# A decoder layer on one core: another interleaving in the order table, fifteen warm-up transposes instead of twenty-five, and one drain less

## The reference

```python
x = layernorm(x + attn(x))        # causal: softmax(q k / sqrt(16)) v, with biases, then Wo, bo
x = layernorm(x + xattn(x, ctx))  # 64 context tokens, key mask from batch 0's lengths
x = layernorm(x + ffn(x))         # down(silu(gate(x)) * up(x)), inner width 1024
# ffn: activations rounded to 8 bits by row, weights rounded to -1, 0, 1 with one scale each
```

## Time and profile before

| | us |
|---|---|
| median of 3 executions (864.41 to 867.02) | 865.58 |
| the profiled execution | 864.41 |
| its span, first to last instruction | 862.7 |
| PE busy | 807.5 |
| DVE busy | 674.9 |
| ACT busy | 578.9 |
| POOL busy | 387.2 |

### The profile page before, as it was taken

The page is one execution under the profiler, slowest core; times in us unless marked ns, Lnnn a source line. Parts: engine busy times, 40 slices in busy tenths (PEclk is TensorE's granted clock), DMA queues, the critical chain, the costliest instruction groups (busy, mean ns, idle before and its releaser), DMA issues.

```text
span 862.7 us, 21746 instructions
## 1 busy us (share of the span) xinstructions
PE 807.5 (94%) x8207; PEld 389.9 (45%) x8235; DVE 674.9 (78%) x1179; ACT 578.9 (67%) x759; POOL 387.2 (45%) x621
## 2 busy tenths in 40 slices
PE   7888999999999999999999999999999999999875
PEld 5433334343554434534464344643645443445533
DVE  5899798658967799778998589874898948836698
ACT  2277865467874688555885679756697569964486
POOL 4724465446343257532634544372634603343345
PEclk8899999999999999999999999999999999999999
DMA  7713124301223212201221111130130100010001
GB/s 227 202 40 99 38 62 105 94 2 27 55 53 98 62 37 49 78 1 26 72 66 39 35 53 45 39 86 20 39 85 17 50 2 1 2 50 1 2 2 49
DMA packets 47814, 45.50 MB, mean 53 GB/s; under 512 B 9698, under 2 KB 43874, under 8 KB 47714
## 3 DMA queue, kind: packets, MB, share of 16 engines
q1 hardware_dynamic: 43698, 39.12, 16.4%
q0 software_dynamic: 1536, 3.15, 1.6%
q10 hardware_dynamic: 2480, 1.84, 0.8%
HBM read 14.55 MB, written 4.19 MB: 22 GB/s over the span
## 4 chain that ended last, share of the span: by engine, by line
PE 75%; DVE 12%; ACT 7%; issue 3%; DMA 1%; POOL 1%; SPq 1%; POOLq 0%; DVEq 0%
PE ps L988 14%; PE ps L1003 14%; PE ps L800 10%; PE ps L962 7%; PE ps L815 5%; DVE shift L1317 5%; PE ps L934 4%; PE ps L861 3%; PE ps L946 3%; ACT probs L1106 3%; PE ps L789 2%; PE ps L891 2%; DVE shift_h L1317 2%; PE ps L903 2%; PE ps L886 2%
## 5 line engine op out<-in xcount | busy, mean ns | idle before, releaser
L1106 ACT ACTIVATE probs<-ps 128x1024 f32<-128x1024 f32 (+3 forms) x384 | 296.2, 810 | 123.6 <-PE ps L988 121.3
L1317 DVE TENSOR_REDUCE shift<-ps 128x2 f32<-128x1024 f32 (+2 forms) x224 | 248.6, 1144 | 51.3 <-PE ps L962 28.8
L988 PE MATMUL ps<-q_stack,k_stack 64*128 64x512 bf16 (+3 forms) x1536 | 174.4, 325 | 10.4 <-ACT probs L1106 3.3
L1003 PE MATMUL ps<-probs,v_aug 128*32 128x512 f32 (+3 forms) x1536 | 155.7, 495 | 0.1
L689 POOL TENSOR_SCALAR_AFFINE_SELECT probs<-probs 128x512 f32<-128x512 f32 x128 | 80.6, 638 | 156.7 <-ACT probs L1106 155.9
L962 PE MATMUL ps<-k_stack,q_stack 64*128 64x512 bf16 (+3 forms) x768 | 115.3, 327 | 9.8 <-ACT probs L1106 3.5
L988 PEld LDWEIGHTS ps<-q_stack,k_stack 64*128 64x128 bf16 x1536 | 54.8, 94 | 121.9 <-ACT probs L1106 45.4
L1317 DVE TENSOR_REDUCE shift_h<-ps 128x4 bf16<-128x512 f32 (+2 forms) x96 | 96.9, 1044 | 15.7 <-PE ps L969 15.2
L962 PEld LDWEIGHTS ps<-k_stack,q_stack 64*128 64x128 bf16 x768 | 39.6, 94 | 97.7 <-ACT probs L1106 36.3
L1003 PEld LDWEIGHTS ps<-probs,v_aug 128*32 128x32 f32 x1536 | 34.8, 108 | 42.9 <-issue 31.4
L966 PE MATMUL ps<-causal,pick_h 64*128 64x128 bf16 x512 | 53.5, 217 | 0.0
(11 more groups left out here) (186 smaller groups left out, 1376.9 us busy)
## 6 DMA issues: line engine op xcount, KB each, us to landing
q_stack<-part_sb SPq DMA_DIRECT2D x168, 64.0 KB, 2.0
k_stack<-part_sb SPq DMA_DIRECT2D x144, 64.0 KB, 2.1
xT<-in_x_cols SPq DMA_DIRECT2D x8, 512.0 KB, 4.0
xt<-in_x SPq DMA_DIRECT2D x8, 512.0 KB, 3.9
out_x<-xt SPq DMA_DIRECT2D x7, 512.0 KB, 2.9
k_stack<-part_sb POOLq DMA_DIRECT2D x48, 64.0 KB, 2.1
q_stack<-shiftT SPq DMA_DIRECT2D x128, 1.0 KB
q_stack<-part_sb ACTq DMA_DIRECT2D x24, 64.0 KB, 2.5
```

The source lines that it names most:

```text
L988: mm = pe.matmul(ps[:, u.banks[i], 0:BANK - off], k_stack[rows, part, h, kb * P:(kb + 1) * P], q_stack[rows, part, c, h, off:BANK], start= ...
L1003: mm = pe.matmul(ps[DV * i:DV * (i + 1), SUM_BANK, off:BANK], v_aug[:, kb, at:at + DV], probs_of(b, n)[:, i, :], start=first, stop=last)
L1106: act.activation(probs_of(b, n)[:, 2 * p:2 * p + 2, :], pair(u)[:, :, 0:BANK - off], ACT.Exp).then_inc(probs_ready, 1)
L1317: dve.tensor_reduce(to[:, :, pairs[0]:pairs[-1] + 1, qb % TH], pair(u)[:, :, 0:len(pairs) * w].rearrange("p j (h w) -> p j h w", w=w), AX. ...
```

## The change

Three edits. The string `ORDER` is replaced by another interleaving of the same 1917 units; 793 of the 1212 units that write banks get other banks. `stir` runs 15 transposes instead of 25. The `pool.drain()` behind `make_masks` is gone. Of the string only the first line stands here:

```diff
 ORDER = (
-    "ffwr6sfffr0sgr6sr1r0r6sr2m01m45m23r6ggm45m01m23m45r6ffffm01m23gr4m01m56m23a01a45am01a23w6a45m01fffaa23a45am2"
+    "r6sr5sr6sr5r6sgr5m01gm23m45r6m01ggm45m01r6fm23m01m23wfm01m45r3fm01a45w6r3m01a45fffam23m01a45w6a23afm45fa01oa"
...
                         make_masks()
-                        pool.drain()
...
                     if b == 0 and u.idx == 0:
-                        stir(u, 25)
+                        stir(u, 15)
```

More of the change, by code:

```diff
@@ L47 @@
[L47 to L66, removed]
@@ new lines @@
+    "am45r6m01ooa23m45a01o23m45sa01om23a45m01a23a45m01oa23m01a45ga23m01a45m23oam01wa45oa23aa01oa45rm23am01a45a23a"
+    "m45a23m01a45gam23om01m45m23r6m01oom23oa45m01ra23o45am01a23a45oaa23m45a01m23goom01awa45oa23aa01m45r6rm01m23a4"
+    "5aa01om45m23a01o01oaa23m45a01em23eaa01m45oa23m01ooogm45a23o01m45a23p01om23m45bm01p6p5a01a23a45opm01m23r6m01p"
+    "a45a23om45rp01m23m45p6m01m23p5pp6p1p0a23bgaop6gm45a01pr3p6p5a01p2p6aa34a01op6m01p24arm01r6m01ra23p45p02p45r6"
+    "p45a01p23m01aa45op23p01a45om23p01om45a23m01p6m23oa01m45p6o01a23a45oa01goa23pm45rm01r6a23m45a01ppaoa23pa45pap"
@@ new lines @@
+    "rom01m23r6a01a45oaa01m23a45p01m45aom23p6m01m45p3p2om01oop6m45gp3o01p2p6p5p3p2a01gpa34m56apr2xppgp1p0a34a56op"
+    "m12aa34a56pppar0p45a23p6p1oa45apa23a01m45ppr6pam01p23p5p6a23a01m45ooop6aa23a01po45aoa23oopa01ppm23p45p6m01p2"
+    "3p6p3papp01otoa45a23m01p6xo45m01ea23p6a23pa01a45oa23om01a45a23pa01m45oam23p45m01a23m45p6m01m23p5pp6p1p0a23op"
+    "6aa23pm45ba01am23a01p6p1p0a23oap6a23m45a01op6oom01p24om01r6m01p23p04rp23r6a23p01p45m01a23p45rp01o23om45p01om"
+    "23a01m45p6m01m23a45p6a01a23gopa45pa01am23m45a23m01m45a23apoa01a23aa45poa01pm23paa45m01r6m23oom01p45m23a01m45"
@@ new lines @@
+    "p6m23op1gm45ap0m23orp6m45p1p0m23p6o45p1p0a23p6m45a01paoa23a45ppapp6p1a23a45ar0pa23pm45oom01prpa23om45aor6o01"
+    "p23p5p6a01m23a45m01aa23a45goapa23m01a45pppop23m45p6p1ap0a45oopoa23pppp01p6ro45m23oa45m01p23p6m45p3ppa01a45p6"
+    "p3p2p01oca45m01p6m23p5pa01a23gm45oa01pm23r6m01a45aa23ora45am01p23om45a01m23p6a01m23p5pp6tp3aa01p2a45ap6a01m4"
+    "5opea23m01oooa45p6p3a01p2a45p6o01a23p6gm45p02m45r6m45p01p24rbp01op01m23p45m01a23p45a01p23om45p01m23om45a01p6"
+    "m01a23am45p6a01m23a45poapa01a23m45r6am01a23m45a23gom01paa23oa45pm23opaopm01m45rr6a23ga01m45p23m01om45m23p6p1"
@@ new lines @@
+    "r0xp5p6p1m23m45p6ap0o23p1p6p5m23a01ooa45aa23a01appppp6m45a23ga01ap6oopa45pppop23p6p1pr0a45par6ppo23p45p1p6a2"
+    "3m45a01ap6a23m01pa45oaa45a23pm01om45oppp23m01p6om45m23xp01p6a45p1ppp23oa45a01m23p6p5o01pa23oa45a01om23pa45oa"
+    "01am23a45om01a23p45am01om23m01p6m23m01p5pp6p3p2a01a45oaa01p6m45pa23m01aoa23a45tp6p1p0a23p6m45r1ep6m23bop04rm"
+    "23r6p01rp24p01r6op01p23a45o01op23a01gp45a23m01p45orm23a45m01p6m23a45m01p6a23m01a45poaa23pm01a45aoa23a45oam23"
+    "a01a45m01aga45pa23pr6m01apm23m45oa01opom23oa45m01ap23m45a01a23rp6m01m23m45p1p0ap6p3o12m45p0p6gp2p3p5a01oa23a"
@@ new lines @@
+    "a45ppppp6p1m23poa45oaa01oa23poppp45p6p1am23r6a01a45pppapgp23p6o01p5oa01p6a45aa23pa01pom45ppom23p01op6om45a23"
+    "p01p6m45ro23oa01m45p6ppa01a45p6p3p2p01cooa01m45p6a01m23p5a01pa23apr6tm01a23a45aoa23m01a45m23m01aa45oa45p23ao"
+    "m01m45a23p6em01m23ba45p6pp5p3p2oa01p6oroa45m23m01pr6ro23a45p1p6p0a23p5om23a01a45p6op02a45oogp01p24p01r6p01a2"
+    "3ap45m01a23p45a01p23aa45m01a23p45oam23m45m01p6p5a01a23grpoaa01m23a45pr6aa01m45a23om01aopa23oa45apr6a01o23a45"
+    "oopm01m45aga23opa01m45p23aom01a45m23m01oa45p6p3m45p2m01o45p6p3ap2m01m45p6p3p2a01p6a45oapom23a01a45ppapp6m01a"
@@ new lines @@
+    "45oa23p6a45pa01pppm23r6p01op5oa23p6a01o45opa23pm45oppp01p6p3a45p6a01ga23ppopm45opap01m23p6a45m23p01p6a45am23"
+    "a01p6m45a01ppp23oatm01a45ea23p6p5apa23a01om45apa23a01ar6a01m23a45aom01a45oom23p45o01om23m45p6m01m23p5pp6p1p0"
+    "a23aop6a23m45oopa01am23a45p6p1oa23p5ap6a01o23a45aa01p6m45p02m45ooa45p01ap24p01a01p23p45m01a23op45oop01a23a45"
+    "p01o23om45a23bm01p6p5a01a23oa45oa01pm23pa45aoa01a23am45pa01a45apa23a01am45pom01m23a45oa01m45pp23a01om45oop6m"
+    "01p3m45o01p2p6m45p3p1p2p6p5p3a01popa45ppp6p3m01poa23a45pm01ppp23op6p5pa01a23a45pppp01p6ap3p2opa45m23a01apopp"
@@ L80 @@
+    "p01a45p6op01a23aa45p6p1a23papa45a01p6p3p2p45ooa01op6p5ta01o23poa45a01a23a45poa01a23ooaa01p45a23oaa01a45p6aa0"
+    "1ea23p5pp6p3p2oaoboop6o01pu01p6p5p3p2u1p6v23p04uuv6vu23p01p24p01vu6p01up23v45u6u1p23up45v6u5vu3p01v6v5u3p2vu"
+    "04v6v3p2u04v6pv02u45pv02u45u01pv23u01v23v45u6ppuv01v6pup01p6vuvvp5p3up2p1up0p6p5up3p2pu23pvppp1p6pu5u3u6vpu2"
+    "pvpu5u1p34p6p5v01uuuppuppp56p3p2v1u0p3u2v0puv6v5v3puppv2p01up6vp45vuvvv3v2u01p6p5vu34vvvpv01u6u5uv01pv6v5vut"
+    "tvt"
 )
```

19 lines of the change are left out of this document (2 added, 17 removed).

## The result

The changed kernel takes 889.55 us (median of 4, 888.61 to 890.96) against 865.9 for the kernel before beside it: a ratio of 1.0275, 95% interval 1.0254 to 1.0297, so 23.8 us slower. Forecast were 861.7 us and a range of 853 to 870.

What follows compares the result with a forecast made beforehand. The limit was taken to change with the stretch (PE or DVE), with 100 us of waits in PE's queue, most hidden. Start -5.25, end +1.4 and middle 0 sum to -3.85, from 865.58 to 861.7 us; range 853 to 870.

Steps and rivals of the forecast that it cites:

- The middle: Batches 0 to 3: reshuffled order with the same work, fewer tight bank hand-backs against closer pv units; 0, bounds 9.3 either way.
- The first rival: Score banks in the middle: direct hand-backs and closer pv units stop PE's queue; slower, 871.0 at the bound; chance 0.2.
- the third rival: Middle: half or all of the 16 fewer tight hand-backs count, -4.7 to -9.3 us, so 857 to 852.4; chance 0.15.
- The drain: Drain removed behind make_masks on POOL: costed at 0, at most 0.1 us either way, hidden by a wait.
- The start: Mask casts moved later, so first rest and first reduction come earlier and the gain carries to the end: -5.25 us.
- the second rival: Low clock at the first projection, +1.6 us, 863.3; or the start's gain swallowed later, 864 to 865.6; chance together 0.25.
- Fifteen transposes: Ten fewer transposes on PE before the first projection: gain 0, since ACT's table load ends just then; clock cost forecast 0.
- The end: Last hquantum waits behind two down takes, 1.7 us later with 0.3 slack: +1.4 us, bounds 0 and +2.5.

Runs made afterwards that it cites:

- order: The kernel before with only the new order table, 25 transposes and the drain kept: 884.24 us, ratio 1.0213.
- the block: Kernel before plus PE-only measuring units behind its last store, each kind alone, then mixed: five mixtures took 0.20 to 0.31 us more per round than their parts.
- fewer_switches: The new order table (25 transposes, drain kept) with 58 neighbour pairs in PE's queue exchanged for fewer changes of unit kind: 905.55 us, ratio 1.0444.
- small: The kernel before with fifteen transposes and no drain behind make_masks, order table untouched: 869.22 us, ratio 1.0031.
- start: The kernel before with its first 130 units in the new order, 25 transposes and drain kept: 867.47 us, ratio 1.0008.
- early: The kernel before with only the mask's casts moved, from place 2 of the list to place 43: 864.84 us, ratio 0.9992.
- a_drain: The changed kernel with its drain behind make_masks put back, fifteen transposes and new order table kept: 885.27 us, ratio 1.0221.
- tail: The kernel before up to unit 1700, the rest in the new order: 867.9 us, ratio 1.0006.

## Why the prediction was wrong

**The middle** (taken as 0, bounds 9.3 either way) is the step that failed. Units 300 to 1690 took 610.5 us with the new table and 595.9 with the old, 15 more; the whole table cost 18.4 us (order), the middle behind the old start 22.2. Two terms of the step were missing or mis-sized. First, the sum had no price for the order itself, "the same work on every engine": each change of the array's shape costs PE 0.10 to 0.16 us, and 59 more of them stand there; that is 6 to 9 us by the block and 9 by the table, more than half of the 15. The step also read the timeline of 575 to 600 us, PE busy for all 25 us, as one stretch among others, and took from the share of the weight loads that PE has over half of the span to give; but from some 150 us on a longer queue of PE lengthened the kernel. Second, the hand-backs of banks were counted in the wrong class. I looked at banks with no unit or one unit of PE between owner and next writer, and found fewer. But of the waits for score and max banks in units 300 to 1690, by my sorting, half stand where two units lie between: 36 of 80, 9.5 of 19.3 us; where one lies between they are 3 with 1.7 us. In order, two between has 47 waits with 15.4 us, one between 8 with 2.8. That class went from 206 to 224 in my own count and was set aside. All late operands and banks together took 7 us more.

**The first rival** had the right sign and place, and 0.2 of chance, but only a small part of the mechanism. Of the two direct hand-backs that it named one lies in the stretch, and it held PE's queue for 1.0 us in order; its bound, 871, was too small, and it has no price for the shape. What direct hand-backs can cost shows fewer_switches, with seven. Its test failed as a test: I had asked for waits for exponentials above 90 us, and they fell to 76.1. The loss shows as waits with no releaser and as longer issue, which that number can't see. By it the third rival, a larger gain, would have been nearly confirmed.

**The drain** (0, at most 0.1 either way) was wrong too: 4.7 us by the ratios 1.0275 and 1.0221, whose intervals allow less than 1 and more than 8; the traces give 1.9 to 3.7 for the same pair and 2.0 in small. It was true that POOL had nothing to do behind `make_masks`, and for that reason the drain was free there. What it did had to be done anyway, and the next drain stood where PE waits. The prediction asked what hides the removed instruction; the question was which later one inherits its work.

**The start**: the first `rest` came at 11.43, as the second rival had it for the low clock, and the casts ran as one block without a wait, near 31, as said. The first reduction at 21.90 was 4.7 us earlier, with the 1.6 of the clock inside. Up to the first score unit the step holds. "It should carry on to the end, since DVE is near its limit right behind" is what failed: the runs start (1.0008) and early (0.9992) show that most of it is given back by 100 us. In early 4.7 of 7.3 us went to the casts and a stretch at the low clock; in the change a projection at the low clock stood there; what took it in start, between 75 and 90 us, no run isolates.

**Fifteen transposes**: order, with 25 of them, has 1.0213, a_drain, with fifteen, 1.0221. The second rival's 1.6 us are in the trace at 10 us and can't be told from zero in the time.

**The end** (+1.4, 0 to 2.5): tail has 1.0006, 0.5 us, with an interval from -0.6 to 1.7: inside the bounds, and not told from zero. The +4 that I read off the two traces was mostly the clock.

What stays open: the 9 us of shape changes rest on the block and on counts, the 7 us of late operands and banks on sorting the traces; no run has taken either out of the new table alone.
